# A Flamingo layer with routed experts: three stage boundaries rearranged, and the routing's table in bf16 parts

## What is computed

```python
x = x + tanh(g_xattn) * attention(layernorm(x), ctx, ctx, mask, w_q, w_k, w_v, w_o, b_o)
x = x + tanh(g_ffn) * moe(layernorm(x), Wg, W1, W3, W2, Ws1, Ws3, Ws2)
# attention: 4 batches of 512 tokens, width 512, 32 query heads in 8 groups, head width 16,
#   causal, scores / 4, softmax, output projection and bias
# moe: scores = softmax(x @ Wg.T) over 16 experts in 4 groups; the 2 groups with the largest
#   maximum stay; the 4 best experts of these get their scores as weights
y = sum_e combine[:, e] * (silu(x @ W1[e].T) * (x @ W3[e].T)) @ W2[e].T      # inner width 352
z = (silu(x @ Ws1.T) * (x @ Ws3.T)) @ Ws2.T                                  # inner width 704
moe = y + z
```

## Time and profile before

| | |
|---|---|
| median of 3 runs | 1331.7 us |
| the profiled execution | 1331.93 us |
| its span in the trace | 1330.1 us, mean granted clock 0.981 |
| ScalarE (ACT) busy | 587.1 us |
| VectorE (DVE) busy | 659.6 us |
| GpSimd (POOL) busy | 639.0 us |
| DMA | 152.92 MB, mean 115 GB/s |

### The profile page before, as it was taken

One profiled execution on the slowest core, in us unless ns is written; L12 is line 12 of the kernel. 1 busy time (PEld: TensorE's weight loads), 2 busy tenths in 40 slices (PEclk: granted clock), 3 DMA queues, 4 the chain that ended last, 5 costly groups with the idle time before them and its releaser, 6 DMA issues. The chain is left out here.

```text
span 1330.1 us, 27215 instructions
## 1 busy us (share of the span) xinstructions
PE 1261.9 (95%) x8457; PEld 923.6 (69%) x8458; DVE 659.6 (50%) x1862; ACT 587.1 (44%) x1018; POOL 639.0 (48%) x726
## 2 busy tenths in 40 slices
PE   7998999999997998999999899999999999999995
PEld 4554544444443345777777589999999999999994
DVE  5345788898896656766424033332353343343300
ACT  1222566666665223321223145555555455555552
POOL 6000333333333323442536256666667766767664
PEclk8998999999998999999999999999999999999998
DMA  9452333333333604000013235555666566665443
GB/s 342 153 161 94 102 109 97 111 93 105 100 108 93 193 32 190 29 36 32 32 40 121 89 73 128 143 136 139 143 144 137 137 155 174 143 158 138 78 72 40
DMA packets 73870, 152.92 MB, mean 115 GB/s; under 512 B 10725, under 2 KB 16357, under 8 KB 73049
## 3 DMA queue, kind: packets, MB, share of 16 engines
q1 hardware_dynamic: 52776, 102.37, 23.5%
q0 software_dynamic: 21040, 49.88, 18.4%
HBM read 97.56 MB, written 52.23 MB: 113 GB/s over the span
## 5 line engine op out<-in xcount | busy, mean ns | idle before, releaser
L208 DVE CUSTOM_DVE_ANT_0 a_mb<-a_mb,late 128x128 f32<-128x128 f32 (+3 forms) x512 | 244.5, 510 | 51.1 <-PE a_mb L189 44.5
L1511 DVE CAST e_w<-e_w 128x480 fp32r<-128x480 f32 x135 | 76.5, 567 | 304.0 <-DMA e_w<-in_w2T 299.8
L640 ACT ACTIVATE a_at<-a_eb 128x1024 f32<-128x1024 f32 (+3 forms) x256 | 179.7, 705 | 103.2 <-PE a_eb L702 102.7
L576 POOL TENSOR_SCALAR_AFFINE_SELECT a_at<-a_at 128x256 f32<-128x256 f32 x256 | 106.0, 415 | 226.1 <-ACT a_at L640 225.9
L1663 PE MATMUL e_yps<-e_w,e_hT 128*128 x711 | 197.3, 404 | 0.9 <-ACT e_hT L1574 0.9
L1642 PE MATMUL e_up<-e_w,e_xT 128*128 x948 | 171.4, 330 | 0.0
L1642 PE MATMUL e_gate<-e_w,e_xT 128*128 x948 | 169.1, 327 | 1.0 <-issue 1.0
L1642 PEld LDWEIGHTS e_gate<-e_w,e_xT 128*128 128x128 f32 x948 | 157.3, 190 | 10.5 <-issue 5.6
L1642 PEld LDWEIGHTS e_up<-e_w,e_xT 128*128 128x128 f32 x948 | 150.6, 190 | 0.0
L1663 PEld LDWEIGHTS e_yps<-e_w,e_hT 128*128 128x128 f32 x711 | 128.1, 189 | 25.5 <-issue 1.2
L189 PE MATMUL a_mb<-a_k,a_q 49*128 49x256 f32 (+2 forms) x512 | 121.1, 426 | 18.7 <-DVE a_mx L208 8.6
(11 more groups left out here) (243 smaller groups left out, 1766.3 us busy)
## 6 DMA issues: line engine op xcount, KB each, us to landing
e_w<-in_w13T SPq DMA_DIRECT2D x16, 1408.0 KB, 6.2
dq<-p_parts SPq DMA_DIRECT2D x32, 256.0 KB, 2.4
a_q<-dq SPq DMA_DIRECT2D x64, 128.0 KB
do<-a_o SPq DMA_DIRECT2D x32, 256.0 KB, 2.1
e_w<-in_w2T SPq DMA_DIRECT2D x16, 512.0 KB, 5.6
a_k<-dk SPq DMA_DIRECT2D x64, 98.0 KB
e_w<-in_ctxT SPq DMA_DIRECT2D x4, 1024.0 KB, 13.8
e_w<-in_x SPq DMA_DIRECT2D x4, 1024.0 KB, 13.5
```

The source lines that it names most:

```text
L208: eng.tensor_tensor_reduce(out=b[:, 0:w], in0=b[:, 0:w], in1=io["late"][:, SEQ - w:SEQ], scale=1.0, scalar=3 * NEG, op0=ALU.add, op1=ALU.m ...
L576: eng.affine_select(out=square, in_=square, compare_op=ALU.is_ge, fill=0.0, base=0, pattern=[[0, 2], [1, P]], channel_multiplier=-1).then_ ...
L640: eng.activation(at[r % 2][:, ch, 2 * hp:2 * hp + 2, ch * P:SEQ], eb[hp][:, :, ch * P:SEQ], ACT.Exp, scale=0.25).then_inc(s_exp, 1)
```

## The change

The three stage boundaries:

1. The last store of the low part of the queries is no longer issued at the end of `stage_project` but as SyncE's first step in `stage_attend`. The second buffer `parts` lies further up in memory, so that the attention's tiles don't cover that part. ScalarE waits at the start of the attention for the first buffer's stores alone.
2. The last store of `o` is issued at the end of `stage_attend` without waiting for its landing; it counts on `s_sums`. `o` lies in the weights' buffer, which outlives the stage. In `stage_close` SyncE loads the heads of batch 1, the gate, `wraw` and the heads of batch 2 first, then waits for that store, and then loads the last batch's sums and the heads of batch 3. VectorE waits for the sums where it did.
3. The experts' first tile is turned in `stage_shared`: `turn_first` stands ahead of `down` for the third block of the last batch, `take_first` ahead of the fourth, and ScalarE makes its two copies there. The last block's residual sum and its store move into `stage_experts`, as VectorE's and SyncE's first steps. Two banks of PSUM and `xT` are shared by both stages.

The table: `put` (token number and weight) is split into bf16 parts, three of the weight and two of the token number, with eight short operations. `at_row` is bf16. `at_tile` goes, and four fused operations of VectorE for each block (compare, times the part) of 5 x 79 elements write `at_col` in bf16. A matmul has 395 columns in place of 158 and is a bf16 product. The parts are added after the last table: one operation more for the index, two more for the scale.

The diff, cut to its core (declarations and renamed operands are left out):

```diff
+        parts.append(sb("p_parts1", [P, KD + 1, 2, SEQ], F32R))
+        io["low_q"] = parts[(BATCH - 1) % 2][:, KD - 1, 1].bitcast(F32)
...
-                    eng.wait_ge(s_qlo, b * KD + i + 2)
-                    eng.dma_start(at[1], parts[b % 2][:, i, 1].bitcast(F32)).then_inc(s_qout[b % 2], 16)
+                    if b * KD + i < BATCH * KD - 1:
+                        eng.wait_ge(s_qlo, b * KD + i + 2)
+                        eng.dma_start(at[1], parts[b % 2][:, i, 1].bitcast(F32)).then_inc(s_qout[b % 2], 16)
...
+            eng.dma_start(dram["q"][NIT - 2:NIT].rearrange("g t r s j n -> s (g t r) (j n)")[1], io["low_q"]).then_inc(io["s_qout"][1], 16)
...
-            store(NIT - 1)
+            eng.wait_ge(s_o, NIT + 1)
+            eng.dma_start(dram["o"][NIT - 1], o).then_inc(io["s_sums"], 16)
...
-            for b in range(2):
-                eng.wait_ge(io["s_qout"][b], 16 * 2 * KD * 2)
-                eng.wait_ge(io["s_kout"][b], 48 * 2)
+            eng.wait_ge(io["s_qout"][0], 16 * 2 * KD * 2)
+            eng.wait_ge(io["s_kout"][0], 48 * 2)
...
-            load_sums(eng, dram, BATCH - 1, BATCH, sums, io["s_sums"])
...
-            for b in range(2, BATCH):
-                load_heads(eng, dram, b, o[b], s_o[b])
+            load_heads(eng, dram, 2, o[2], s_o[2])
+            eng.wait_ge(io["s_sums"], 32)
+            load_sums(eng, dram, BATCH - 1, BATCH, sums, io["s_sums"])
+            load_heads(eng, dram, BATCH - 1, o[BATCH - 1], s_o[BATCH - 1])
...
-            eng.wait_ge(io["s_sums"], 32)
+            eng.wait_ge(io["s_sums"], 48)
...
-        NG, NK = E // EG, TOPK
+        NG, NK, PARTS = E // EG, TOPK, 5
...
+        at_row = [io["rows"][2 + r].bitcast(BF16)[:, 0:NK * P].rearrange("p (k n) -> p k n", k=NK) for r in range(2)]
+        at_col = [sb(f"r_atcol{r}", [P, NK, PARTS, TILES], BF16) for r in range(2)]
+        put = io["rows"][2][:, 256:384].rearrange("p (t k n) -> p t k n", t=NT, k=NK)
+        puts = z[:].rearrange("p t e -> p (t e)").bitcast(BF16)[:, 0:NT * NK * PARTS].rearrange("p (t k n) -> p t k n", t=NT, k=NK)
...
-        tokps = ps("r_tokps", [P, 2 * TILES])
+        tokps = ps("r_tokps", [P, PARTS, TILES])
...
+            for n in range(PARTS):
+                rest = put[:, :, :, n % 2]
+                eng.tensor_copy(puts[:, :, :, n], rest).then_inc(s_v, 1)
+                eng.wait_ge(s_v, next(done))
+                if n + 2 < PARTS:
+                    eng.tensor_tensor(rest, rest, puts[:, :, :, n], ALU.subtract).then_inc(s_v, 1)
+                    eng.wait_ge(s_v, next(done))
...
-                if t:
-                    eng.wait_ge(s_row, 3 * t + 1)
-                eng.tensor_tensor(at_tile[:], iota_g[:].rearrange("p (o g) -> p o g", o=1).broadcast_to([P, NK, TILES]),
-                                  col[:, t, :].rearrange("p (k o) -> p k o", o=1).broadcast_to([P, NK, TILES]), ALU.is_equal).then_inc(s_tile, 1)
-                eng.wait_ge(s_tile, t + 2)
-                for n in range(2):
-                    eng.tensor_tensor(at_col[r][:, :, n, :], at_tile[:],
-                                      put[:, t, :, n:n + 1].broadcast_to([P, NK, TILES]), ALU.mult).then_inc(s_row, 1)
+                for k in range(NK):
+                    eng.scalar_tensor_tensor(out=at_col[r][:, k], in0=iota_g[:].rearrange("p (o g) -> p o g", o=1).broadcast_to([P, PARTS, TILES]),
+                                             scalar=col[:, t, k:k + 1], in1=puts[:, t, k, :].rearrange("p (n o) -> p n o", o=1).broadcast_to([P, PARTS, TILES]),
+                                             op0=ALU.is_equal, op1=ALU.mult).then_inc(s_row, 1)
...
-            eng.tensor_scalar(indexf[:], tokps[:, 0:TILES], pad[:, 0:1], None, ALU.add).then_inc(s_v, 1)
+            eng.tensor_scalar(indexf[:], tokps[:, 1, :], pad[:, 0:1], None, ALU.add).then_inc(s_v, 1)
+            eng.wait_ge(s_v, next(done))
+            eng.tensor_tensor(indexf[:], indexf[:], tokps[:, 3, :], ALU.add).then_inc(s_v, 1)
...
+            eng.tensor_copy(scale, tokps[:, 0, :]).then_inc(s_v, 1)
+            eng.wait_ge(s_v, next(done))
+            for n in (2, 4):
+                eng.tensor_tensor(scale, scale, tokps[:, n, :], ALU.add).then_inc(s_v, 1)
+                eng.wait_ge(s_v, next(done))
...
-            eng.wait_ge(s_down, NT + 1)
-            last = x1[BATCH - 1][:, CH - 1, :]
-            eng.scalar_tensor_tensor(out=last, in0=yps[(NT - 1) % 2][:], scalar=tg[:, 0:1], in1=last,
-                                     op0=ALU.mult, op1=ALU.add).then_inc(s_v, 1)
-            compared.append(next(done))
...
+                        if b == BATCH - 1 and j == 1:
+                            eng.wait_ge(s_turned, 2)
+                            eng.activation(io["x0"][:, 0], xps, ACT.Copy).then_inc(s_x0high, 1)
+            eng.wait_ge(s_turned, 3)
+            eng.activation(io["x0"][:, 1], xps, ACT.Copy).then_inc(s_x0high, 1)
...
+            def turn_first():
+                eng.wait_ge(io["s_rows"][0], 16)
+                eng.wait_ge(s_v, compared[0])
+                for k in range(KD):
+                    mm = eng.matmul(xps[:, k, :], io["rows"][0][:, k * P:(k + 1) * P], io["ident"], is_transpose=True, start=k == 0, stop=False,
+                                    skip_group_check=True)
+                mm.then_inc(s_turned, 1)
+
+            def take_first():
+                eng.wait_ge(s_x0high, 2)
+                eng.matmul(io["xps"], io["lessr"], io["x0"][:, 0].rearrange("p k n -> p (k n)"), start=False, stop=True,
+                           skip_group_check=True).then_inc(s_turned, 1)
+
...
-                eng.wait_ge(s_row, 3 * t + 4)
+                eng.wait_ge(s_row, (NK + 1) * (t + 1) + 1)
...
+                        if b == BATCH - 1 and j == 2:
+                            turn_first()
+                        if b == BATCH - 1 and j == 3:
+                            take_first()
...
+        xT = [io["x0"], io["x1"]]
+        last = residual(io, BATCH - 1)[:, CH - 1, :]
...
+            eng.wait_ge(s_last, 7)
+            eng.dma_start(out[bass.ts(NT - 1, P), :], last).then_inc(io["s_base"], 16)
...
+            eng.scalar_tensor_tensor(out=last, in0=io["last_y"], scalar=io["tg"][:, 0:1], in1=last,
+                                     op0=ALU.mult, op1=ALU.add).then_inc(s_last, 1)
...
-            part_x(0, 0)
...
-            eng.wait_ge(s_pad, 3)
-            turn_x(0, 0, 0)
-            take_high(0, 0)
...
+        for i in range(2):
+            io[f"x{i}"] = io["ws"][:, i * 2 * KD * P:(i + 1) * 2 * KD * P].rearrange("p (m k n) -> p m k n", m=2, k=KD)
+        io["tg"] = sb("k_tg", [P, 1])[:]
+        io["xps"], io["last_y"] = (c.enter_context(nc.psum_tensor(f"k_{n}", [P, D], F32))[:] for n in ("xps", "last_y"))
```

More of the change, by code:

```diff
@@ L230, in stage_project @@
         sem = dsem = lambda n: c.enter_context(nc.semaphore(n))
-        parts = [sb(f"p_parts{i}", [P, KD + 1, 2, SEQ], F32R) for i in range(2)]
+        parts = [sb("p_parts0", [P, KD + 1, 2, SEQ], F32R)]
         wq, wk, wv = sb("wq", [P, KD, D]), sb("wk", [P, KD, P]), sb("wv", [P, KD, P])
@@ L1208, in _ @@
             eng.wait_ge(s_v, next(done))
-            eng.tensor_tensor(put[:, :, :, 0], rows(tok[:].rearrange("p (t o) -> p t o", o=1), NK), row[:], ALU.subtract).then_inc(s_v, 1)
+            eng.tensor_tensor(put[:, :, :, 1], rows(tok[:].rearrange("p (t o) -> p t o", o=1), NK), row[:], ALU.subtract).then_inc(s_v, 1)
             eng.wait_ge(s_v, next(done))
+            for n in range(PARTS):
[5 more added lines that the diff above has]
+                    eng.wait_ge(s_v, next(done))
             for t in range(NT):
@@ L1377, in down @@
                         first = its * DOWN + n * D
-                        mm = eng.matmul(yps[i % 2][:], h[0:size, mine, n, j * P:(j + 1) * P],
+                        mm = eng.matmul(yps[i % 2], h[0:size, mine, n, j * P:(j + 1) * P],
                                         io["w"][0:size, bass.ds(side[1], 1), first:first + D].rearrange("p b n -> p (b n)"),
@@ L1455, in stage_experts @@
         x = io["rows"]
-        xT = [sb(f"e_xT{i}", [P, 2, KD, P], F32R) for i in range(2)]
+        xT = [io["x0"], io["x1"]]
+        last = residual(io, BATCH - 1)[:, CH - 1, :]
         act = [sb(f"e_act{i}", [P, INTER]) for i in range(2)]
```

59 lines of the change are left out of this document (29 added, 30 removed).

## The result

The changed kernel takes **1344.0 us** (median of 4 runs, 1343.16 to 1346.02) where the kernel before measures 1331.5 beside it: a ratio of 1.0094, 95% interval 1.0073 to 1.0114. It is slower by 12.6 us, and the forecast was 1328.9 with a range that ended at 1334. The profiled execution took 1343.16 us; its span is 1341.4 against 1330.1, its mean granted clock 0.973 against 0.981.

The account below looks back on a forecast made before the run. TensorE, busy 1261.9 of 1330.1 us, was taken as the bound. First seam -0.6, second +3.3, table -3.0 and third -2.5 sum to -2.8; 1331.93 - 2.8 - 0.2 = 1328.9 us, range 1322 to 1334.

Parts of the forecast that it names:

- The table: Routing's table in the shared expert: cheaper bf16 matmuls, partly lost waiting for VectorE; -3.0 us, ends -6.1 and +0.5.
- The text's own formula: Table: time from one group's begin to the end of the next, 8.6 us with a VectorE pair of 6.9.
- Rival (b): Table: VectorE becomes its bound, nothing comes out of it, the rest as forecast; 1331.9 us, no change; chance 0.15.
- end of -1.8: Table: its value in us if both GpSimd operations block VectorE in full, 7.6 us a pair.
- The second seam: Attention to close: sums land about 440.5 us behind weights, TensorE idles, low clock follows; +3.3 us, ends -3.4 and +6.8.
- +1.0: Second seam: the late sums eat TensorE's slack of 6.5 us and 1.0 us more, low clock not counted.
- 447.1 of the text: Second seam: time in us when batch 1's first normalisation, which TensorE needs for `widen(1, 2)`, would end.
- the clock's 2.3: Second seam: cost in us of some 5 us at the lower clock after TensorE's new idle time.
- +6.8: Second seam: its bad end in us, with the sums landing at 442.9; +3.4 and another +3.4.
- rival (c): Second seam: sums land at 442 or later, long low clock, table -1.5; +2.2, at worst 1334.8 us; chance 0.13.
- Rival (a): Second seam: sums land early or their wait is hidden, seam -1.6; whole -7.7, 1324.0 us; chance 0.27.
- First and third seam: First: last DMA issue leaves the chain, -0.6 us; third: shorter idle and low stretch before the experts, -2.5 us.

Follow-up runs that it names:

- run 10: The kernel before with the first seam's edit alone: 1326.9 us, ratio 0.9967.
- run 4: The kernel before with the second seam's edit alone: 1338.8 us, ratio 1.0067.
- run 3: The kernel before with the bf16 table alone: 1340.8 us, ratio 1.0079.
- run 11: The kernel before with the third seam's edit alone: 1327.7 us, ratio 0.9966.
- run 6: The changed kernel with GpSimd's product and subtraction cut to 8 of 512 columns in the table's eight units (result not the layer's): 1328.2 us, ratio 0.9975.
- run 1: The changed kernel with the last batch's sums loaded right behind the heads of batch 1, ahead of the weights: 1332.6 us, ratio 1.0021.
- run 12: The changed kernel with GpSimd's four subtractions in the close waiting until VectorE has split the last reciprocals: 1341.5 us, ratio 1.0071.
- run 5: The changed kernel with the sums loaded early and the float32 table of before: 1323.8 us, ratio 0.9948.
- run 7: Run 1 with one table in most units, two in three of them, and the gathers moved to the second last unit: 1323.6 us, ratio 0.9931.
- run 9: Run 7 with the four gathers issued behind GpSimd's last unit: 1319.2 us, ratio 0.9907.
- run 8: The changed kernel with 85 products of 128 columns, whose result nobody reads, ahead of the stalled `widen(1, 2)`: 1341.3 us, ratio 1.0080.

## Why the prediction was wrong, point by point

**The sum.** By ratios the four parts measure -4.4 (run 10), +8.9 (run 4), +10.5 (run 3) and -4.5 (run 11): +10.5 together, beside the +12.5 of the whole, no more apart than the intervals allow. The forecast had, in the same order, -0.6, +3.3, -3.0 and -2.5.

**The table is the step that failed**, with the wrong sign. Two terms were mis-sized, one was missing.
- A fused operation's cadence was put at 0.48 us; run 6 shows four in 2.17 with nothing beside them, 0.54. Eight make 0.5 us a pair.
- What GpSimd costs a pair was taken over from before, 1.84 us for two operations; it is 3.0. In the rows above three of the eight fused operations are longer by 1.0 us each, two in the first tile and one in the second: the pair now lasts longer than a unit, and so meets a third operation of GpSimd, the next unit's. Together 8.6 us in place of 6.9, with 6.86 to spend. The text's own formula, 0.9 + 8.6 + 0.1 + 0.7, gives 10.3 from one begin to the end of the next group; the trace has 10.2 (603.51 to 613.71). So the mechanism was right, and with the right sizes it would have said a loss of 2 us: four pairs of groups at 10.3 - 5.44 make 19.4 in place of 17.4. The trace has -6.0 + 7.8 = +1.8.
- The missing term made the larger part of the loss. Rival (b) priced a VectorE bound at no change, as if a wait of 1.9 us cost 1.9. Behind three of the four waits the clock fell to its lower level (630 to 636 in the windows above; 668 to 670 and 686 to 688 read 0.50 as well), and that cost another 5.7 us in the trace. It isn't the same each time: in run 1's trace, with the same waits, the stage takes 230.0 us in place of 235.3. For the seams the working did book a low stretch behind an idle time; inside the shared expert it booked none.

The Trainium skill (SBUF — State Buffer, Who interferes with whom) says that a VectorE instruction with two inputs in SBUF contends with a GpSimd one that reads SBUF, and that the later one waits for the whole of the other. The prediction gave that the end of -1.8 and took a value of -3.0; the runs are on the rule's side. The three long fused operations end at 606.68, 608.79 and 613.10, each 0.42 to 0.44 us behind the end of the GpSimd operation that they began beside. Run 6 shows 3.0 us a pair, and run 12 brings the operation that took 2.17 back to 0.69. Where VectorE came first, GpSimd's product took 1.80 us (604.44, behind the compare that began at 604.40) where it took 1.27 before.

**The second seam had the right mechanism and too small a size.** The shape is as forecast: the sums behind the weights, a wait of VectorE, a wait of TensorE at `widen(1, 2)`, the low clock. The landing was guessed at 440.5 with the attention ending where it did before, 17.9 us after its end; it came 19.0 after. (The text's own 442.9 less two is 440.9, which would have made the +1.0 a +1.4.) The split's 2.1 us beside GpSimd were not in the sum at all: the same edit issues `wraw` at 424.67 instead of 429.18, so that GpSimd's four subtractions begin at 437.90 and no longer at 444.41, while the reciprocals moved the other way, and the two met. Counted from the attention's end, 1.1 + 2.1 is all but 0.1 us of the difference between the 447.1 of the text and the trace's 447.89. So +1.0 became +4.3, and the clock's 2.3 is 2.2 in the trace. The upper end, +6.8, and rival (c), which used it, are the nearest to the 8.9 measured; (c) had 0.13, and it was taken together with a small gain of the table, never with a loss. Rival (a) is what runs 1 and 5 bring about: its mechanism holds, the loss of the seam goes when the landing is early. Whether a gain of 1.6 is left of that seam the times can't tell: -6.9 for all three against -8.9 for the first and the third. By run 5's trace 1.1 is left: `widen(1, 2)` begins 22.4 us after the attention's end, at 439.36, where it began 23.5 after it.

The Trainium skill (DMA: Bandwidth & Descriptors, Queues, rings and completion order) was cited for a load whose landing can't come before what its DMA engines took earlier. The trace agrees: 64 KB took 11.0 us behind the weights, 5.0 ahead of them with the heads of batch 1 in front, 1.9 at the head of the queue.

**First and third seam** went the right way and further. The idle times were forecast at 2.9, 2.5 and 2.4 us and are 2.45, 2.37 and 2.66. At the first, -0.6 became -1.05 in one trace and -1.08 in the other, more than the 0.54 us of the issue; what else went there the runs don't show. At the third the idle term (-1.6, the added TensorE work included) was sound: -2.4 + 0.9 in the changed kernel, -2.5 in run 11. The low stretch behind it, booked at -0.9, goes with the experts' 3.3 us in run 11 and 1.6 in the changed kernel, but run 10 has 2.2 there without the edit.

**The range.** It held the bad end of one part at a time. Here both parts with a wait in them came out badly together: the table far past its end of +0.5, the second seam about at its own of +6.8 (+6.5 in the changed kernel's trace, +8.9 with an interval of 6.4 to 11.6 by run 4). They share two causes: VectorE beside GpSimd, and the clock behind TensorE's waits.

## What to carry to other kernels

An idle time of the bounding engine has two prices, its length and the lower clock behind it: price each new wait with both, a short one inside a busy stage too. Before moving a load, read how many bytes stand ahead of it in its queue, and before shortening TensorE's side of a pipeline, compare the feeding engine's time, measured beside its neighbours, with the new period; where it is within a few per cent, spread the work over more periods, as runs 7 and 9 do. When a wait goes or comes, look also at which engine's work slides under which other's.

## What the runs showed of the hardware

- A wait of 1.94 us in TensorE's stream was followed by 6 us at 1.2 GHz (630 to 636 above), though not each time: behind the one at 613.16 the windows up to 628 read 1.00. Four of them cost 7.8 us of waiting, and 15.8 us of time by run 6. Over the 100 us with the four, three traces read a granted clock of 0.93 and two read 0.98.
- Beside GpSimd's tensor operations VectorE's short ones stretch from 0.42 to 1.06 (CAST) and from 0.69 to 2.17 us (TENSOR_TENSOR), and go back when GpSimd is made to wait (run 12). GpSimd's four subtractions there keep their length, 7.28 and 7.13, but its product in the shared expert takes 1.80 us in place of 1.27 where VectorE's compare began just before it.
- A bf16 matmul of 395 columns comes every 0.178 us at the full clock, as estimated: a group of eight adds 6.86 - 5.44 = 1.42 us. That is 11.4 us for 64, against 17.4 for the 128 float32 instructions of 158 columns, 6.0 less; run 6 shows 4.8 of it in the time.
- 85 products whose result nobody reads, put into a wait of TensorE, kept the clock up (run 8): 1.00 behind it where it was 0.50.
